# A convolution-attention layer and a gated mixture on one core: weights prepared by rows, image 0 first, half-packed pair 0, and a new division of the work at the end

## The reference

```python
x = x + L0(_gn(x), ...)      # _gn: group norm, 32 groups of 3 channels
x = x + L1(_gn(x), ...)

# L0
qkv = einsum('bchw,oc->bohw', x, w_qkv)            # 288 x 96
qkv = depthwise 3x3 convolution of qkv with w_dw, padding SAME
q, k, v = split(qkv); 8 heads of 12 channels; q, k = l2norm over the 256 points
attn = softmax(einsum('bhdn,bhen->bhde', q, k) * temperature)
out = einsum('bhde,bhen->bhdn', attn, v);  out = einsum('bchw,oc->bohw', out, w_proj)

# L1
scores = softmax(x_flat @ gate_w + gate_b)         # 4 experts
top_v, top_i = top_k(scores, 2);  top_w = softmax(top_v)
coef[e] = (is e first choice of any token) * top_w[0] + (second choice of any token) * top_w[1]
y[e] = w2[e] @ relu(w1[e] @ x + b1[e]) + b2[e];  out = sum over e of y[e] * coef[e]
```

## Time and profile before

| | |
|---|---|
| median of 3 runs | 169.04 us (168.91 to 170.16) |
| profiled execution | 170.19 us, span 168.4 us |
| granted TensorE clock | 0.99 |
| busy: PE / DVE / ACT / POOL | 148.9 / 144.0 / 101.4 / 45.4 us |

### The profile page before, as it was taken

How to read it: one execution, slowest core, us unless ns; L and a number is a source line. 1 busy time by engine, 2 the same in 40 slices (tenths; PEclk the granted TensorE clock), 3 DMA queues, 4 the chain that set the end, 5 groups by cost and what they waited for, 6 DMA issues and landing times.

```text
span 168.4 us, 3554 instructions
## 1 busy us (share of the span) xinstructions
PE 148.9 (88%) x1275; PEld 118.6 (70%) x1275; DVE 144.0 (86%) x389; ACT 101.4 (60%) x227; POOL 45.4 (27%) x63
## 2 busy tenths in 40 slices
PE   0486896999998999999999899898999798999963
PEld 0476795999998999999999899675674242333322
DVE  2579999877999999999799699659779999999992
ACT  3075087565928639379399147485499768675710
POOL 5130220540514235425246225451227000000000
PEclk9999999699999999999999999999999999999999
DMA  6994305041140410503204100000000000112313
GB/s 151 226 232 103 70 0 157 6 134 26 38 124 0 133 29 0 155 9 85 76 2 117 44 0 6 0 0 2 4 0 0 0 0 0 47 47 58 90 47 93
DMA packets 8810, 9.72 MB, mean 58 GB/s; under 512 B 3640, under 2 KB 7512, under 8 KB 8792
## 3 DMA queue, kind: packets, MB, share of 16 engines
q1 hardware_dynamic: 8648, 9.25, 21.8%
q10 hardware_dynamic: 144, 0.24, 0.4%
HBM read 2.94 MB, written 1.57 MB: 27 GB/s over the span
## 4 chain that ended last, share of the span: by engine, by line
PE 44%; DVE 42%; issue 7%; DMA 2%; ACT 2%; POOL 1%; DVEq 0%; POOLq 0%
DVE v_acc L1136 9%; PE qk_ps L720 8%; PE qk_ps L722 8%; DVE h_mixed L1395 5%; PE out_ps L809 4%; DVE stats L1092 3%; PE sc_ps L774 3%; PE sc_ps L784 3%; PE qk_ps L725 3%; DMA x_sb<-in_x 2%; PE v_ps L766 2%; DVE wc L1021 2%; DVE x_sb L1403 2%; PE small_ps L826 2%; PE v_ps L969 2%
## 5 line engine op out<-in xcount | busy, mean ns | idle before, releaser
L1136 DVE SCALAR_TENSOR_TENSOR v_acc<-v_ps,v_taps,v_acc 96x576 f32<-96x576 f32 x64 | 51.8, 809 | 1.2
L720 PE MATMUL qk_ps<-w_a,x_a 128*128 128x192 f16 x243 | 46.6, 245 | 0.0
L722 PE MATMUL qk_ps<-w_b,x_b 128*128 128x192 f16 x243 | 46.5, 245 | 0.0
L720 PEld LDWEIGHTS qk_ps<-w_a,x_a 128*128 128x128 f16 x243 | 24.6, 101 | 0.2
L722 PEld LDWEIGHTS qk_ps<-w_b,x_b 128*128 128x128 f16 x243 | 23.6, 97 | 0.3
L527 ACT ACTIVATE h_mixed<-qk_ps,slope 128x512 f32<-128x512 f32 x24 | 16.9, 775 | 5.4 <-PE qk_ps L946 5.3
L725 PE MATMUL qk_ps<-w_c,x_c 96*128 96x192 f16 x81 | 20.1, 248 | 0.0
L479 ACT ACTIVATE sc_exp<-sc_qk,neg_max 96x12 f32<-96x12 f32 x16 | 4.7, 296 | 21.3 <-DVE neg_max L1175 21.3
L640 POOL TENSOR_TENSOR sq_sum<-qk_sq 128x384 f32<-128x384 f32 x8 | 8.0, 1002 | 32.8 <-ACT qk_sq L441 25.1
L1395 DVE TENSOR_TENSOR h_mixed<-h_mixed,hidden 128x512 f32<-128x512 f32 x24 | 15.0, 679 | 0.0
L1092 DVE BATCH_NORM_STATS2 stats<-x_sb 96x6 f32<-96x256 f32 x32 | 11.7, 412 | 3.0 <-DMA x_sb<-in_x 2.8
(11 more groups left out here) (200 smaller groups left out, 349.9 us busy)
## 6 DMA issues: line engine op xcount, KB each, us to landing
x_b<-x_a SPq DMA_DIRECT2D x7, 324.0 KB, 3.1
x_sb<-in_x SPq DMA_DIRECT2D x8, 192.0 KB, 4.8
out<-xs SPq DMA_DIRECT2D x7, 192.0 KB, 2.1
x_a<-x_lo SPq DMA_DIRECT2D x7, 108.0 KB, 2.7
x_b<-x_lo SPq DMA_DIRECT2D x7, 108.0 KB, 2.5
x_c<-x_lo SPq DMA_DIRECT2D x21, 36.0 KB, 1.9
wdw_all<-in_L_conv_w_dw SPq DMA_DIRECT2D x1, 648.0 KB, 6.3
w_sb<-in_L_conv_w SPq DMA_DIRECT2D x2, 144.0 KB
```

Source lines behind the costliest of these rows:

```text
L720: eng.matmul(to, window(x_a[p][:, dx, b], half, dy), w_a[:, t, :], start=(t == 0), stop=False, skip_group_check=True)
L722: mm = eng.matmul(to, window(x_b[p][:, dx, b], half, dy), w_b[:, t, :], start=False, stop=False, skip_group_check=True)
L1136: eng.scalar_tensor_tensor(out=v_acc[i % 3][:, :, :], in0=v_window(dy, dx), scalar=v_taps[:, t:t + 1], in1=v_acc[i % 3][:, :, :], op0=ALU. ...
```

## The change

What changes in each part:

- The taps of q and k are multiplied into rows of w_qkv (output channels on partitions), and the products are turned: 18 transposes of 96x96 into five banks. VectorE makes taps 0 to 5 in two products, ScalarE taps 6 to 8 in six copies with a scale. Rounding goes in five groups of two taps (one in the last). `wdw_all` and its transfer of 648 KB are gone. w_v is scaled and turned by itself.
- Image 0 is normalised, cast, subtracted and shifted ahead of image 1. TensorE convolves tile 0 after projecting v of image 0, and projects v of image 1 after that tile.
- Tiles 2 and 3 of pair 0 (image 1) are packed: its six transfers, of one image, follow the weights' five on SP. The loads of pairs 3 to 7 come behind them.
- w_proj is turned in turn 1, w1 in turn 5, w2 in turn 6; `prep_w1` is in turn 4 and `low_w1` in turn 5 on VectorE. Constants in bfloat16 are made by ScalarE and GpSimd at the start.
- Chain 3 has one pair, chain 4 four; the statistics of pair 5 come in turn 2, of 6 and 7 in turn 3.
- The gate's product stands after tile 3 in turns 5 and 6, and for pair 2 after `gram(7)`.
- ScalarE copies qk_ps ahead of the centre tap and squares it behind. It rectifies blocks 2 and 6 too.
- Comparisons: six, each expert against those before it (>=) and behind it (>), written straight into `beaten`, whose diagonal GpSimd cleared.
- Bias and b2: ScalarE makes a tile of it (`bias_tile`), GpSimd adds it to x_sb; VectorE only adds the product. The spread weights of even pairs go to out_ps. `weight(0)` comes ahead of `first(21)`; scores of chunk 1 come after two mixings, their split after the third, and their turn inside `second(2)`. The last product takes its three parts as they come, in two halves each.
- Fewer filler matmuls: two at the start instead of nine, none before `second(0)` instead of three.
- `ONE_TAP` is empty, so `other_tap` and `add_tap` are not called.

```diff
-CHAIN_COLS = [(0, 2), (2, 6), (6, 10), (10, 16), (16, 20), (20, 24), (24, 26), (26, 30), (30, 32)]
+CHAIN_COLS = [(0, 2), (2, 6), (6, 10), (10, 12), (12, 20), (20, 24), (24, 26), (26, 30), (30, 32)]
-RELU_DVE = (2, 6, 18, 20, 22)
+RELU_DVE = (18, 20, 22)
+ONE_TAP = ()
...
-        w0_ps = hid_ps[0:2]
+        w0_ps = [out_ps[:, :], hid_ps[0]]
+        y_last = [v_bank[1], hid_ps[1]]
+        wc_ps = [qk_ps[0], sc_ps, out_ps, mix_ps, qk_ps[1]]
...
# SP
+                b = slice(1 if i == 0 else 0, 2)
+                eng.dma_start(x_b[p][0:C, :, b], x_a[p][0:C, :, b]).then_inc(packed[p], 16)
...
-            for i in range(3, PAIRS):
-                load(i)
-            eng.wait_ge(wc_hi_set, 3)
+            eng.wait_ge(wc_hi_set, 5)
...
+            pack(0)
+            for i in range(3, PAIRS):
+                load(i)
# ScalarE
+            def last_taps(first, last):
+                eng.wait_ge(dw_set, 1)
+                for t in range(first, last):
+                    for s in range(2):
+                        a = eng.activation(wc[:, t, s * C:(s + 1) * C], wqkv_sb[:, s, :], ACT.Copy,
+                                           scale=dw_scaled[:, t, s:s + 1])
+                    a.then_inc(wc_last, 1)
...
+            def bias_tile(i):
+                wait(eng, x1_biased, i - 1)
+                eng.activation(b2_part[i % 2][:, :], w0_ps[i % 2][0:C, :], ACT.Identity, scale=bias_col[:, 0:1],
+                               bias=bias_col[:, 1:2]).then_inc(b2_ready, 1)
...
             coefs(1)
+            bias_tile(0)
+            bias_tile(1)
+            top_exps(1)
+            for i in range(2, PAIRS):
+                if i == 4:
+                    take_u(1)
                 coefs(i)
+                bias_tile(i)
# GpSimd, at the end
+            for i in range(PAIRS):
+                eng.wait_ge(b2_ready, i + 1)
+                eng.tensor_tensor(x_sb[:, i, :], x_sb[:, i, :], b2_part[i % 2][:, :], ALU.add).then_inc(x1_biased, 1)
# TensorE
-                if i == 0 or i == 1 and n == 0:
+                if i == 0 and n < 2 or i == 1 and n == 0:
...
+                    if first == 0 and i == 0 and n == 2:
                         eng.wait_ge(w_packed, 16 * 5)
...
             def weight(i):
-                if i < 2:
-                    wait_hidden_taken(eng, HT - 4 + i)
+                if i == 0:
+                    eng.wait_ge(x1_done, PAIRS)
+                elif i == 1:
+                    wait_hidden_taken(eng, HT - 4)
                 else:
                     eng.wait_ge(coef_set, MT * (i - 1))
-                    eng.wait_ge(x1_biased, i - 1)
+                    eng.wait_ge(b2_ready, i - 1)
...
                 for m in range(MT):
+                    if i == 2 and m == 2:
+                        turn_u(1)
# VectorE
+            def combine(first, last):
+                n = last - first
+                eng.wait_ge(dw_set, 1)
+                eng.tensor_tensor(wc[:, first:last, :].rearrange("p t (s c) -> p t s c", s=2),
+                                  wqkv_sb[:, 0:2, :].unsqueeze(1).broadcast_to([C, n, 2, C]),
+                                  dw_scaled[:, first:last, :].unsqueeze(3).broadcast_to([C, n, 2, C]), ALU.mult)\
+                   .then_inc(wc_set, 1)
...
+                for e in range(EXPERTS):
+                    own = g_exp[:, t, e:e + 1]
+                    if e > 0:
+                        b = eng.tensor_tensor(pairs[:, :, e, 0:e], g_exp[:, t, 0:e], own.broadcast_to([128, n, e]),
+                                              ALU.is_ge)
+                    if e + 1 < EXPERTS:
+                        b = eng.tensor_tensor(pairs[:, :, e, e + 1:EXPERTS], g_exp[:, t, e + 1:EXPERTS],
+                                              own.broadcast_to([128, n, EXPERTS - 1 - e]), ALU.is_gt)
...
             gate_rank(0)
             gate_present(0)
+            add_eps(8)
             gate_scores(0)
+            make_shift(8)
+            gate_weights(0)
+            gate_split(0)
             take_logits(5, 3)
             gate_logits(1)
-            gate_weights(0)
-            gate_split(0)
...
             mix(0)
-            add_bias(0)
-            gate_weights(1)
-            gate_split(1)
-            mix(1)
-            add_bias(1)
-            add(0)
-            for i in range(2, PAIRS):
+            mix(1)
+            gate_scores(1)
+            add(0)
+            mix(2)
+            gate_weights(1)
+            gate_split(1)
+            add(1)
+            for i in range(3, PAIRS):
                 mix(i)
-                add_bias(i)
                 add(i - 1)
```

More of the change, by code:

```diff
@@ L901, in _ @@
             norm_vars(7)
+            first(5)
             first(6)
@@ L951, in _ @@
             weight(0)
-            first(23)
-            weight(1)
+            first(21)
+            first(22)
             eng.wait_ge(cols_step, 2)
@@ L956, in _ @@
                .then_inc(bias_done, 1)
+            first(23)
+            weight(1)
             def second(i):
```

479 lines of the change are left out of this document (286 added, 193 removed).

## The result

The changed kernel takes **180.06 us** (median of 4 runs, 179.80 to 180.40); the kernel before took 169.08 beside it (168.91 to 170.16). The ratio is 1.064, with a 95% interval of 1.060 to 1.068. The forecast was 165.4, a gain, with a range up to 169.0; it was wrong in sign, and by 14.7 us. The profiled execution has a span of 178.0 us (168.4 before) and a granted TensorE clock of 0.971 (0.990 before).

A forecast was written before the change was run, and what follows sets the result against it. The chain of waits was split almost evenly between TensorE and VectorE, each holding different stretches. Gains of 3.9 + 0.7 - 1.0 = 3.6 us off the 169.04 median gave 165.4 us, range 162.5 to 169.0.

The forecast's parts named there:

- 3.9 + 0.7 - 1.0 = 3.6 us: Whole kernel: 3.9 us gained in start and turns, 0.7 in the middle, 1.0 lost in the end.
- TensorE waits 0.5 in turn 4 and 0.95 in turn 5: Turns 4 and 5: means of eight columns, w1's preparation and the key norms' spread put VectorE behind, costing those waits.
- fill idle time, and what they might do to the clock is in the range: Start: filler matmuls cut from TensorE got no term of their own; any clock effect was left to the range.
- the wait for the packing: Start, ahead of tile 2 of pair 0: TensorE idle some 3.3 us for packed x, half clock behind taken as 1.6.
- rival 2: Start swallowed: 1.15 us products, full half clock, 1 us wait in turn 1 for pair 1's packing; 167.9 us, chance 0.2.
- 0.5 + 0.95 + 0.65 = 2.1: Turns 4 to 6: TensorE's waits of 0.5 and 0.95 us, plus 0.65 for transposes of w1 and w2.
- waits of the gate and the gate of pair 2: Turns 6 and 7: gating products moved save twice 0.6 us of waiting; pair 2's gate leaving turn 7 saves 0.86.
- 0.7 gained, 1.3 without a block: Middle: first mixing 1.3 us earlier if GpSimd's subtraction does not block the scores, 0.1 if it does; 0.7 taken.
- The ring: Middle: VectorE waits for ScalarE's exponential before chunk 1's logits, for which ScalarE waits in turn, 1.3 us.
- rival 4: Trios of taps or bias tiles don't overlap; ScalarE, without a gap from 119 to 137, takes the work; 168.0 us, chance 0.08.
- rival 3: End: GpSimd's additions stop a VectorE mixing in every pair, 3.61 us a pair against TensorE's 3.07; 171.3 us, chance 0.12.
- Against it is the phase worked out above: End: GpSimd's addition starts when ScalarE's bias tile ends and overlaps the next mixing only 0.1 to 0.2 us, inside 0.6 slack.

The follow-up runs named there:

- experiment 15: The kernel before with the six small comparisons instead of two wide ones, a product and a sum, nothing else of the change: 169.35 us, ratio 0.996.

## Why the prediction was wrong, step by step

By stretch the forecast was 3.9 + 0.7 - 1.0 = 3.6 us gained; the trace has -1.7, -4.05 and -3.8. That is 13.1 us. Most of the other 1.6, 1.4, comes from the profiled executions (that of before lay 1.15 above its median, that of after 0.26 below).

**Waits were priced at their own length. This is the step that failed, the largest of four.** "TensorE waits 0.5 in turn 4 and 0.95 in turn 5" was right in sum, 1.45 us at one place in turn 5, and in part by luck: up to 0.67 of it is the block by GpSimd, which the prediction didn't have there. But I gave a wait a half clock only at pair 0, where the trace of before showed one, and let every other wait cost itself. In turn 5 the half clock cost 3.0 us more: 39.1 us from the projection of pair 5 to the first product with w1, against 36.1 in the trace with the logits moved, which has the same code up to there, the same wait and a full clock. In the middle it cost 1.7. These 4.7 us are not enough for the sign: at full clock the change loses 4.7 us where 3.6 were to be gained.

**The start.** The pieces were sized well: the new product took 0.75 us (0.67 forecast), the first tile began at 12.51 (12.2). The cut fillers "fill idle time, and what they might do to the clock is in the range": it was in no term of the sum. Tiles 0 and 1 ran at 160 ns, which ate the lead, and hid the wait for the packing; in the nine packed traces where the rate rose in time, the wait is there (0.59 to 3.91 us), and in the four of 1.84 us or more the half clock too. The clock of turn 1 stayed full, so turn 2 began 1.66 us ahead (37.59 against 39.25), not 3.1; at turn 4 it was 2.5, not 3.95. The wait in turn 1 for the packing of pair 1, from rival 2, is there too when the projection is early: 0.24 to 0.71 us at 30 us in four traces.

**w1 in turns 4 to 6** was charged 0.5 + 0.95 + 0.65 = 2.1. That is what turns 4 to 7 show at full clock: from the projection of pair 4 to the first product with w1, 47.65 us against 45.60 with w1 early. But early it costs 0.6 in turn 1, so moving it loses only 1.5 (79.4 against 77.9 us for the turns). The other edits of these turns (waits of the gate and the gate of pair 2) were to gain 2.06 and gain 1.26: 45.60 us against 46.86 before.

**The middle.** "0.7 gained, 1.3 without a block" was 4.05 lost. The ring stood in the text, with 1.3 us for ScalarE's wait; it was 2.35. The top differences are there at 127.2 and ScalarE comes to their exponential at 130.49, behind the last normalisation, two casts and two rectifications, which I had not walked through. The comparisons gave what was forecast on VectorE (0.95 a chunk, against 0.9), but only 1.13 of 1.9 us on the path. With the ring undone, the middle of the change takes 30.2 to 30.3 us, as before, but the scores of chunk 1 have left it. With the scores back in it, it takes 31.38, against 29.16 in the kernel before with the comparisons alone: its other edits cost 2.2 us. Of these, 0.5 is more work of TensorE (27.89 and 28.38 us busy) and the rest its idle time. Which edit it was, was not tried. ScalarE was not without a gap, as rival 4 had it; it waited for VectorE.

**The end is rival 3**, given 0.12. The period of a pair is 3.50 us (3.61 forecast there), and the stretch 3.8 longer. "Against it is the phase worked out above" failed: in the last four pairs the addition falls into the mixing. In the rows above it starts at 164.67, 0.74 us after the first mixing, and not with the last one's end. What sets this phase was not tried. Of the 3.8, GpSimd's additions are 3.0, the new order 2.0 (1.5 of them the scores that came from the middle), and the last product gives 1.2 back. The Trainium skill (SBUF — State Buffer, Who interferes with whom) has a VectorE instruction with two SBUF inputs and a GpSimd one that reads SBUF exclude each other; the traces agree, with mixings of 884 instead of 679 ns in the mean, and 681 once GpSimd is out.

**The whole.** The 13.1 us between the forecast and the traces are: half clocks 4.7, GpSimd's additions 3.0, the ring 2.4, the lead at turn 4 (2.5, not 3.95) 1.4, the rest of turns 4 to 7 1.1, the rest of the middle 0.6, and 0.2 back in the rest of the end. Rival 3 alone gives 171.3, 2.2 under the executions with a full clock (173.5). No rival had a half clock outside pair 0. A rival "the new waits in turn 5 and the middle are each followed by one" belonged there: by the 2.1 us of the earlier trace rows it adds 4.2.

## What to carry to other kernels

When an edit gives TensorE a new wait among dense matmuls, price it twice: its length, and its length plus the half clock behind it (1.7 to 3.1 us here; 0.5 where VectorE held the chain), and give the second a chance of its own. Where an engine waits for a result that stands deep in another's in-order queue, walk the ring to its end before you move anything ahead of it. When you cut a run into stretches, see which work an edit carries over the cut. Work given to GpSimd was not free beside a stream of VectorE's products of two SBUF operands; here it cost more than doing it on VectorE.

## What the runs showed of the hardware

- Waits of TensorE in the 17 traces, and the clock in the 5 us from their end. Of 23 waits of 1.41 to 1.59 us, six were followed by half clock (0.66 to 0.68 granted in the mean), 17 not (1.00); of the eight at one place of the same code, in turn 5, two. All nine of 1.84 to 3.91 us were (0.50 to 0.68), though three executions at a mean clock of 1.00, of which there is no trace, must have passed the place of one of 2.37 without it. None of the 40 of 0.9 to 1.3 us was. The Trainium skill (TensorE: Matmul & The Clock Gate, HAM oscillation — how this bites in real kernels) has a wait on a DMA between bursts of matmuls bring half rate; the runs agree for the long waits, whichever engine they are for, and show it now and then for those of about 1.5 us.
- Before the rate first rises the granted clock reads 1.00 while the matmuls run at 160 ns. In the changed kernel's first trace the 18 transposes of 96x96 and some 60 matmuls with 96 rows ran at the low rate up to 25.6 us, though TensorE had no wait after 7.5. In the kernel before, with its nine fillers of 128x128, the rate is full at 13.4 in one trace, and in experiment 15, with the same start, only at 17.3. What decides it was not separated.
- GpSimd's addition of 512 columns takes 1.26 to 2.79 us in the end (1.56 in the mean), where its subtraction of as many takes 1.17 in the mean.
